# Two chosen experts of a token, in fifteen sorted tiles, in place of all eight

## The reference

```python
x = x + _L0_attn_ref(_layernorm(x), ...)
x = x + _L0_xattn_ref(_layernorm(x), ctx_1024, ctx_1024, mask, ...)
# _L0_ffn_ref, on z = _layernorm(x); E = 8, K = 2, D = 128, FF = 512
attn_out = ao @ Wo + bo
x1 = _layernorm(z + attn_out, g1, be1)
gate_probs = jax.nn.softmax(x1 @ Wg + bg, axis=-1)
topk_p, topk_i = jax.lax.top_k(gate_probs, K)
topk_p = topk_p / jnp.sum(topk_p, axis=-1, keepdims=True)
comb = jnp.sum(jax.nn.one_hot(topk_i, E) * topk_p[..., None], axis=-2)
h = jax.nn.gelu(jnp.einsum('bsd,edf->bsef', x1, W1) + b1, approximate=False)
y = jnp.einsum('bsef,efd->bsed', h, W2) + b2
moe_out = jnp.einsum('bse,bsed->bsd', comb, y)
return _layernorm(x1 + moe_out, g2, be2)
```

## Time and profile before

| what | value |
|---|---|
| median of three runs | 814.39 us |
| the profiled execution's own time | 816.61 us |
| its span, on which all rows count | 814.8 us |
| PE busy | 757.1 us, 93% |
| DVE, ACT, POOL busy | 427.1, 355.5, 95.7 us |
| mean granted TensorE clock | 0.98 of 2.4 GHz |
| DMA over the span | 19.92 MB, mean 24 GB/s |

### The profile page before, as it was taken

One profiled execution on the slowest core, in us unless ns is written; L12 is line 12 of the kernel. 1 busy time (PEld: TensorE's weight loads), 2 busy tenths in 40 slices (PEclk: granted clock), 3 DMA queues, 4 the chain that ended last, 5 costly groups with the idle time before them and its releaser, 6 DMA issues.

```text
span 814.8 us, 9092 instructions
## 1 busy us (share of the span) xinstructions
PE 757.1 (93%) x3433; PEld 389.4 (48%) x3433; DVE 427.1 (52%) x1021; ACT 355.5 (44%) x492; POOL 95.7 (12%) x87
## 2 busy tenths in 40 slices
PE   4889899998999999999999999999999999988995
PEld 2654654366644443465544443466543443333433
DVE  4564477646733677447544678356444577132102
ACT  0315026753242457743442467742542367632431
POOL 4100100001002100020122100020122000022111
PEclk9999999999999999999999999999999999998997
DMA  6800000000000000010000000000010000001010
GB/s 173 246 1 0 1 0 2 0 8 26 1 14 26 27 13 1 1 46 14 1 27 26 26 14 1 1 14 14 0 41 13 27 14 1 0 27 35 32 37 26
DMA packets 18212, 19.92 MB, mean 24 GB/s; under 512 B 1730, under 2 KB 11224, under 8 KB 18168
## 3 DMA queue, kind: packets, MB, share of 16 engines
q1 hardware_dynamic: 18168, 19.34, 8.0%
HBM read 18.22 MB, written 1.11 MB: 24 GB/s over the span
## 4 chain that ended last, share of the span: by engine, by line
PE 82%; DVE 9%; issue 4%; ACT 3%; POOL 1%; SPq 0%; DMA 0%; POOLq 0%; DVEq 0%; ACTq 0%
PE banks L1055 13%; PE banks L1044 13%; PE banks L1405 8%; PE banks L1032 7%; PE banks L1373 6%; PE banks L1395 4%; DVE nm L952 2%; PE banks L1266 2%; PE banks L1269 2%; PE banks L1356 2%; PE banks L1297 2%; PE banks L1295 2%; PE banks L1078 2%; PE banks L1314 1%; PE banks L1308 1%
## 5 line engine op out<-in xcount | busy, mean ns | idle before, releaser
L952 DVE TENSOR_REDUCE nm<-banks 128x1 fp32r<-128x512 f32 x256 | 160.0, 683 | 39.4 <-PE banks L1373 39.2
L525 ACT ACTIVATE hT<-banks,cols 128x512 f32<-128x512 f32 x128 | 87.9, 687 | 178.1 <-PE banks L1044 178.0
L656 ACT ACTIVATE px<-banks 128x1024 f32<-128x1024 f32 x128 | 125.5, 1023 | 41.4 <-PE banks L1395 41.0
L1044 PE MATMUL banks<-x1T,w 128*128 128x512 f32 x256 | 137.4, 622 | 1.9 <-ACT hT L525 1.0
L1055 PE MATMUL banks<-hT,w 128*128 128x512 f32 x256 | 135.6, 613 | 3.6 <-DVE ys L713 2.9
L1032 PE MATMUL banks<-sel_r,eye_r 128*128 128x512 f32 x244 | 81.3, 432 | 5.0 <-DVE nm L952 4.0
L1055 PEld LDWEIGHTS banks<-hT,w 128*128 128x128 f32 x256 | 47.9, 194 | 71.2 <-issue 49.9
L713 DVE TENSOR_TENSOR ys<-banks,combB 128x512 f32<-128x512 f32 x32 | 22.1, 692 | 113.0 <-PE banks L1055 112.9
L1373 PE MATMUL banks<-kst,qst 32*128 32x512 f32 x256 | 69.2, 470 | 1.0 <-ACT kst L629 0.8
L1044 PEld LDWEIGHTS banks<-x1T,w 128*128 128x128 f32 x256 | 46.0, 196 | 49.8 <-issue 40.9
L1405 PE MATMUL banks<-px,vf 128*32 128x512 f32 x512 | 68.2, 604 | 1.4 <-ACT px L656 0.7
(11 more groups left out here) (230 smaller groups left out, 903.4 us busy)
## 6 DMA issues: line engine op xcount, KB each, us to landing
combB<-gate_weights SPq DMA_DIRECT2D x32, 256.0 KB, 3.1
w<-in_L_ffn_W SPq DMA_DIRECT2D x1, 2048.0 KB, 9.7
msk<-in_mask SPq DMA_DIRECT2D x4, 308.0 KB, 3.6
xin<-in_x SPq DMA_DIRECT2D x4, 256.0 KB, 2.9
ot<-in_const_sel SPq DMA_DIRECT2D x1, 1024.0 KB
out<-outb SPq DMA_DIRECT2D x4, 256.0 KB, 2.3
cos<-in_const_cos SPq DMA_DIRECT2D x1, 256.0 KB
sin<-in_const_sin SPq DMA_DIRECT2D x1, 256.0 KB
```

The costliest lines, as they stand in the source:

```text
L525: act.activation(hT[:, j % 2, :], bank[h_bank(j)], ACT.Gelu, bias=cols[:, ROW_B1 + j:ROW_B1 + j + 1]).then_inc(k["h_act"], 1)
L656: act.activation(px[:, c % 2, 2 * i:2 * i + 2, :], banks[:, 4 + 2 * i:6 + 2 * i, :], ACT.Exp, scale=SCALE_H).then_inc(k["f_exp"], 1)
L952: dve.tensor_reduce(nm[:, t, g, BLK * hh:BLK * hh + 1], bank[s1_bank(g, t, hh)], AX.X, ALU.max, negate=True).then_inc(k["f_max"], 1)
L1044: pe.matmul(bank[h_bank(j)], w1[:, e, c * P:(c + 1) * P], x1T[:, p % 2, :], start=True, stop=True).then_inc(k["h_ready"], 1)
```

## The change

The experts of batch p now see only the tokens that chose them. A token has two of them, so 1024 rows are sorted by expert into tiles of 128 rows, each of one expert; 15 tiles (`NT`) hold every split.

- DVE's gate has 25 steps in place of 17 (`gate_step`): it makes marks (a one for each chosen expert), PE counts with them (`gate_ranks`, five small bf16 matmuls) how many earlier tokens chose the same expert, and DVE works out each token's row (`slot`) and each tile's expert (`eid`). They stand behind the units of the first part of `cross(p+1)` (`GATE_AT`), no longer in the second part. The last one is behind unit 14 of 0 to 15.
- POOL scatters the tokens with 8 indirect DMAs (`send_tokens`) to rows of DRAM, SP loads the tiles back (`load_tokens`, four DMAs), PE turns them (`turn_tokens`, 15 transposes) and ACT scales and copies them (`tokens_turned`, four).
- `turn_tokens` stands behind `project_heads` in the third part of `cross(p+1)`. The gaps w0, w1 and w2 are empty; w3 to w6 take 6 tiles, the o gaps 2, the t gaps 4, the x gaps 3.
- `up` is four matmuls of 128 columns and 128 tokens, `down` four, for one tile; ACT does four gelus of 128 columns per tile. DVE adds `b2` once per four tiles (`add_biases`).
- The experts' weights no longer lie in SBUF: SP reads the tile's expert from `eid` and loads 526 KB of weights (`wp`, five slots) and a spread row of `b2` per tile (`load_expert`), a slot when the tile five before is done.
- The results go to DRAM (`keep_y`, four DMAs), POOL gathers them with 8 indirect DMAs (`fetch_tokens`), DVE mixes both by their gate weights (`end_step`, 8 operations), and the last layer norm follows, now in the third part of `cross`.
- Gone: `comb`, its turn and its DMAs, `scale_experts`, `add_experts`, `end_rows`, the loads of `w1` and `w2` at the start. `ln_rows(0)` of the next batch moves from the second to the third part of `cross`, and POOL's add to `x2b` behind `finish`.
- `keep_warm` in the gaps of batches that don't exist falls with the counts, from 44 chunks' worth to 22 tiles' worth, four matmuls each.

```diff
+NT = (2 * S + NE * (P - 1)) // P
+YG = 4
+NG = -(-NT // YG)
+WSLOTS = 5
+OUT_AFTER = 8
+RANKS_AT = 9
-MOE_GAPS = (("w0", 2), ("w1", 2), ("w2", 2), ("w3", 3), ("w4", 2), ("w5a", 2), ("w5b", 2), ("w6", 1), ("w7", 0),
-            ("o0", 1), ("o1", 1), ("o2", 1), ("o3", 1),
-            ("ta", 1), ("tb", 2), ("tc", 2), ("td", 2), ("te", 1), ("tf", 0),
-            ("x0", 1), ("x1", 1), ("x2", 1), ("x3", 1), ("xq", 0))
+MOE_GAPS = (("w0", 0), ("w1", 0), ("w2", 0), ("w3", 2), ("w4", 1), ("w5a", 2), ("w5b", 1), ("w6", 0),
+            ("o0", 1), ("o1", 0), ("o2", 1), ("o3", 0),
+            ("ta", 0), ("tb", 1), ("tc", 1), ("td", 1), ("te", 1), ("tf", 0),
+            ("x0", 1), ("x1", 1), ("x2", 1), ("xq", 0))
...
+            def load_expert(p, i):
+                n = NT * p + i
+                if n >= WSLOTS:
+                    sp.wait_ge(k["y_part"], n - WSLOTS + 1)
+                e = sp.value_load(eid[0:1, p % 2, i:i + 1], min_val=0, max_val=NE - 1)
+                sp.dma_start(wp[:, n % WSLOTS, :],
+                             experts_in[bass.DynSlice(e, 1)].rearrange("e p c -> (e p) c")).then_inc(w_in[n % WSLOTS], 16)
...
+            def send_tokens(p):
+                pool.wait_ge(k["g_slots"], p + 1)
...
+                for j in range(2 * T):
+                    pool.indirect_dma_start(xs_dram, bass.IndirectOffsetOnAxis(slot[:, p % 2, j:j + 1], 0),
+                                            xn[:, p % 2, j % T, :], None).then_inc(k["xs_sent"], 16)
+            def fetch_tokens(p):
+                for i in range(2):
+                    pool.wait_ge(y_kept[i], 16 * (NG // 2) * (p + 1))
...
+                for j in range(2 * T):
+                    pool.indirect_dma_start(yg[:, j // T, j % T, :], None, ys_dram,
+                                            bass.IndirectOffsetOnAxis(slot[:, p % 2, j:j + 1], 0)).then_inc(k["y_back"], 16)
...
             def cross(n):
                 p = n - 1
-                for label in X_GAPS:
-                    add_experts(p - 1, label)
+                if p >= 0:
+                    gate_exp(p)
+                    send_tokens(p)
+                if p >= 1:
+                    fetch_tokens(p - 1)
                 if n + 1 < B:
                     rstd_of(0, n + 1)
...
+                    for c in range(FC):
+                        ins = act.activation(hT[:, n % 2, c * P:(c + 1) * P], bank[h_bank(i)][:, c * P:(c + 1) * P], ACT.Gelu,
+                                             bias=wp[:, n % WSLOTS, 2 * FF + c:2 * FF + c + 1])
...
+                    if p >= 0:
+                        for i in GATE_AT[u]:
+                            gate_step(p, i)
...
-                pe.matmul(bank[h_bank(j)], w1[:, e, c * P:(c + 1) * P], x1T[:, p % 2, :], start=True,
-                          stop=True).then_inc(k["h_ready"], 1)
+                for c in range(FC):
+                    ins = pe.matmul(bank[h_bank(i)][:, c * P:(c + 1) * P], wp[:, n % WSLOTS, c * P:(c + 1) * P],
+                                    xT[:, i * P:(i + 1) * P], start=True, stop=True)
```

575 lines of the change are left out of this document (328 added, 247 removed).

## The result

The changed kernel takes 808.54 us (median of four executions, 803.35 to 821.18), the kernel before 815.14 beside it: a ratio of 0.989, interval 0.985 to 0.992. It is 1.1% faster where 7% were forecast, and 808.5 lies outside the range of 736 to 788. The profiled execution took 807.43 us with a span of 805.6.

A forecast was written before the change was run, and what follows sets the result against it. It took PE (93% busy, 82% of the chain) as the bound, above a floor set by the DVE, ACT and POOL chain. Terms -7 -4 -1.5 -10.5 -6 -22 -5 -0.8 + 0 = -57 gave 758 us; range 742 to 775, widened 736 to 788.

The forecast's parts named there:

- The first parts: First parts of cross attentions: added DVE gate steps lengthen them, cross(1) to 18.2 us (+4.6), cross(2) to 19.7 (+2.6).
- The tails: Four tiles replace eight chunks: tail(1) and tail(2) come to 25.9 us, -3.4 each; tail(3) -4, tail(0) -1.5.
- The price of an indirect DMA on POOL: POOL's 16 indirect DMAs a batch: taken as 1.2 us each, with 0.4 and 3.1 as ends.
- The third parts: Third parts of cross(1) to cross(3): floor chain of 27.6 us plus 2.5 for clock, 30.1; -10.3, -10.8 and -10.8.
- To this comes the clock. ... I add 2.5: Third parts of cross: thinner PE work brings a fall to half clock on the path, 2.5 us each.
- -3.3 for each of three: Second attentions of batches 1 to 3: two tiles (3.6 us) replace four chunks (6.9), -3.3 us each.
- With the first one, -0.5: First second attention, self_attention(0): a gain of only 0.5 us, from 65.7 to 65.2.
- half clock in all thinned stretches: Rival: PE at half clock in every new third part and tail, 10 us a batch, 788 in all; chance 0.13.
- so they cost nothing up to 1.8 us each: Indirect DMAs in cross(2): POOL is through at 38.9, the layer-norm power is wanted at 48.6, so no cost.
- The end: Behind the last logits: saved chunks (55 us) come back as a chain of DMAs; 92.0 us against 92.2, no gain.
- The rival of late weights: Slot reloads not overlapped: ten tiles at the end take 5 us each, +27, 785 in all; chance 0.12.
- The rival of slow indirect DMAs: Indirect DMAs hold POOL longer, growing the end, cross(2) and cross(3): 777 at 2.0 us, 827 at 3.1; chance 0.10.

The follow-up runs named there:

- mid3: late_warm with the mixing back in its old place and gathers started once three of four copies of the sums are out; 757.3 us, ratio 0.928.
- warm_o0: Changed kernel with eight warming matmuls put back in gaps o1 and o3 of the first second attention; 797.7 us, ratio 0.973.
- warm_o_end: Changed kernel with warming in o1 and o3 of all four second attentions and 68 warming matmuls at the end; 795.9 us, ratio 0.974.
- all_four: apart, plus batch 2's last gathers waiting for batch 3's token reload, plus warming matmuls in the third parts; 784.2 us, ratio 0.961.
- before_thin: Kernel before the change, without eight warming matmuls in gaps o1 and o3 of self_attention(0); median 827.5 us, ratio 1.003.
- gather_late: Changed kernel with the gathers moved behind both layer-norm powers and the mixing behind the rotation; 824.1 us median.
- plain_gather: Changed kernel with the eight gathers as plain DMAs from POOL's queue, sorting back left out; 802.9 us.
- scatter_plain: Changed kernel with plain scatters (no sorting), indirect gathers in their place, and warming in o1 and o3; 768.2 us in one execution.
- mid2: As mid3, but the gathers start behind the second copy of the sums; 758.9 us, ratio 0.928.
- apart: warm_o_end without its 68 end matmuls; SP waits for the gathers before reloading sorted tokens and weights; 785.4 us, ratio 0.964.
- late_warm: gather_late with warming matmuls in o1 and o3 of the second attentions and in the third parts; 781.5 us, ratio 0.958.
- light_weights: Changed kernel loading only the last 4 of 1028 weight columns from the last batch's sixth tile on; 795.8 us in one execution.

## Why the prediction was wrong

**What held.** The tile: eight products in 1.78 us, read from start to start of two tiles of the changed kernel in cross(1):

```profile
259.73 1.05 PE L1191 MATMUL banks<-xT,wp 128*128 128x128 f32 x8
260.62 1.06 PE L1202 MATMUL banks<-wp,hT 128*128 128x128 f32 x8
261.51 1.06 PE L1191 MATMUL banks<-xT,wp 128*128 128x128 f32 x8
```

The first parts: 16.4 (forecast 18.2) and 19.3 (19.7). The tails: 24.5 against 25.9. tail(0) lost warming and is down to 24.5 as well, so the 25.9 that was taken for the floor was in part its warming. The price of an indirect DMA on POOL, 1.2: the page's groups for scatter and gather show 0.976 and 0.952, and 0.30 between two, 1.25 in all.

```profile
L540 POOL DMA_INDIRECT expert_tokens<-xn,slot x32 | 31.2, 976 | 53.2 <-DVE slot L991 44.7
L550 POOL DMA_INDIRECT yg<-expert_rows,slot x32 | 30.5, 952 | 39.3 <-DMA expert_rows<-xs 29.8
```

**What came right for another reason.** The third parts took 27.2, 29.9 and 29.0 us where 30.1 was forecast for each: a chain of 27.6, of which 3.4 were the end of batch p-1, and 2.5 for the clock. cross(1) has no batch p-1 to end, so its chain was 24.2 and is 3 us longer than worked out; in its timeline ACT's copy for the second split (L723) starts at 265.4, right behind the gelus of the last of three tiles, which the sum left out. In cross(2) that end came on time, 23.4 us behind the sums (forecast 23.6), but the two splits behind it (L1079) took 3.1 us (438.5 to 441.6) for the 1.4 of the sum. And the fall of the clock was not where the 2.5 were charged. The third part of cross(2) up to 440.4, its last 4 us, and the third part of cross(2) in mid3 (that of cross(3), too, has 1.00):

```profile
414.60:440.40 25.80, 20.30 (x144) 16.80 (x143) 19.76 (x61) 12.95 (x33) 5.53 (x5) 1.00 0.29 82
440.40:444.50 4.10, 2.08 (x5) 1.16 (x6) 1.88 (x2) 0.69 (x1) 3.94 (x4) 0.50 0.87 260
...
389.40:419.24 29.84, 25.34 (x165) 19.84 (x163) 21.58 (x62) 13.61 (x34) 15.99 (x15) 1.00 0.44 131
```

So the third part has nearly its whole length at the full clock too (29.9 against 29.0 in cross(3) is what the last 4 us at 0.50 can have cost), and that 30.1 fits is luck.

**The step that failed first: the clock.** The prediction said: "To this comes the clock. ... I add 2.5", for each third part. It charged the fall where PE would idle, and took its length, 3 us, from the earlier trace rows. The fall came behind the third parts, in the second attentions, where the prediction had "-3.3 for each of three" and "With the first one, -0.5": with no term for the clock in either. Measured: 27 us at 0.50 in self_attention(0), and 10, 20 and 17 us in the other three or just ahead of them, 30.0 us lost against the forecast. That warming in the emptied gaps brings the clock back is shown by warm_o0 for the first one and by warm_o_end with all_four for the others; before_thin speaks for it without the rest of the change, by its scatter only. The rival "half clock in all thinned stretches" named the mechanism but priced it at "10 us a batch" for third part and tail, and gave it 0.13; it left out the second attentions. tail(1) and tail(2) kept their clock, and tail(0) and tail(3), at 0.93 and 0.95, came near their forecasts. The length of 3 us rests on the single fall of the earlier trace rows; in the scores and stacks of self_attention(0) 1.2 GHz stayed for 27 us here and for 78 in gather_late.

The Trainium skill (TensorE: Matmul & The Clock Gate, Part 1) says that activity releases the throttle. The rows of gather_late don't agree: PE is busy for 30.00 of 30.00 us and stays at 0.50. What decides is open here; that a measured fall of 3 us isn't an upper bound for the next one is shown.

**The second: "so they cost nothing up to 1.8 us each".** That step asked only when POOL would be free, and the answer was right: the power was not late. It took for granted that an issuing POOL leaves DVE and ACT alone. The gathers right behind the scatters cost 9.6 and 9.8 us in the second parts of cross(2) and cross(3), of the 11.0 that each of those stages should have gained. Shown: in this place the stall goes when the gathers are plain (plain_gather), when the scatters are (scatter_plain), and when the gathers start 5.6 or 10.2 us behind the scatters (mid2, mid3); it does not need SP's traffic (apart). Not shown: whether it is the unbroken row of sixteen or the place of the gathers against the sums, as no run has eight gathers alone start between the first and the second sums; by what path DVE and ACT are held up; and why the sixteen at the end of mid3 do no harm. A break alone is not the rule: in late_warm, 21 us behind the scatters, the rotation of cross(2) still came 3.9 us behind its first projection, 0.2 behind the eighth gather, and in all_four the gelus at the end were late 8 us behind the scatters.

The Trainium skill (SBUF — State Buffer, section "SBUF: two separate sides") names one shared pair of ports, of DVE and GpSimd, and says that ACT never waits on anyone. The trace shows ACT 11.9 us late beside DVE's 7.1, so that port cannot be the whole explanation.

**The end.** Forecast 92.0, measured 97.6. The first `up` came 35.2 us behind the logits (forecast 32.3), as ACT's copies of the turned tokens waited beside the gathers of batch 2. The first four tiles took 10.4 us, the first 4.4 of them at 0.50 (forecast 7.2), the other eleven 2.40 each (2.3). The last part, 25.6, was 25.3 in the forecast. The rival of late weights had the right place, and light_weights its size: 4.3 us, not 27. The rival of slow indirect DMAs was priced at 827 for 3.1 us each; by its own formula it is 830.

**As a sum.** The forecast's span, 757.8, plus 30.0 for the second attentions, 17.3 for cross(2) and cross(3), 5.6 for the end, 0.7 each for cross(0) and the start, less 4.4 for cross(1) and 2.4 for the tails, gives 805.3; the span is 805.6. With both causes removed mid3 takes 757.3. That this is the forecast's number is in part luck: its tails are shorter and its second attentions longer (68.5 against 66.6, about the 1.9 us of its own warming) than forecast, and 3 us of it are a start that the edits don't touch.

The trade shows in the mean granted clock, which was 0.980, 0.898 and 0.962 of spans of 814.8, 805.6 and 754.4 us: 33 us at 1.2 GHz in the kernel before, 164 in the changed one and 57 in mid3, 47 of which are the end.
